# A memset of 256 spare words behind each gather on GpSimd, in the keys-and-values stage and in the gate stage of a graph network

## What is computed

```python
# layer 1, attention: per edge
k_e = k[src] + angle_emb @ We ; v_e = v[src] + angle_emb @ We
alpha = einsum('ehd,ehd->eh', q[dst], k_e) / sqrt(D)       # 8 heads of 16
# ... softmax over the edges of each target, then the sum of attn * v_e by target
# layer 3, gates: per edge
gates = softmax(concat([x_src, x_dst, x_edge]) @ W_gate + b_gate)
out = gates[:, 0:1] * x_src + gates[:, 1:2] * x_dst + gates[:, 2:3] * x_edge
segment_sum(out, col, num_segments=N)
```

## Time and profile before

| | |
|---|---|
| median of three runs | 7083.06 us (7050.15 to 7134.01) |
| span of the profiled execution | 7080.9 us; no other time of that execution is given |
| keys-and-values stage, first to last gather | 2370.6 to 3800.4 us |
| gate stage, first to last gather | 5607.2 to 7013.9 us |
| busy shares of the span | TensorE 59%, VectorE 42%, GpSimd 41%, ScalarE 18% |

### The profile page before, as it was taken

The page is one execution under the profiler, slowest core; times in us unless marked ns, Lnnn a source line. Parts: engine busy times, 40 slices in busy tenths (PEclk is TensorE's granted clock), DMA queues, the critical chain, the costliest instruction groups (busy, mean ns, idle before and its releaser), DMA issues.

```text
span 7080.9 us, 98147 instructions
## 1 busy us (share of the span) xinstructions
PE 4162.5 (59%) x25513; PEld 3308.9 (47%) x25514; DVE 2977.6 (42%) x8318; ACT 1295.5 (18%) x3253; POOL 2894.8 (41%) x2784
## 2 busy tenths in 40 slices
PE   1112000599898455555563664798899666666664
PEld 1001000366565455555553563465565666556654
DVE  3438201411313344444446677212312555555556
ACT  0001000000100211111111664200200322322222
POOL 6778777000000265555553565000000255555555
PEclk6555555799899777777776996899999755655555
DMA  9713000366463455555552451464364222222222
GB/s 361 267 61 135 6 0 0 103 198 192 141 195 118 111 160 158 154 150 156 155 162 89 125 148 30 137 197 138 131 196 145 64 78 78 78 78 79 79 78 69
DMA packets 447985, 885.48 MB, mean 125 GB/s; under 512 B 91722, under 2 KB 278572, under 8 KB 441502
## 3 DMA queue, kind: packets, MB, share of 16 engines
q1 hardware_dynamic: 333406, 608.36, 27.1%
q0 software_dynamic: 106912, 224.30, 11.9%
q10 hardware_dynamic: 7584, 51.91, 2.0%
HBM read 728.93 MB, written 155.35 MB: 125 GB/s over the span
## 4 chain that ended last, share of the span: by engine, by line
PE 33%; DVE 20%; issue 19%; another core or an unknown queue 15%; DVEq 6%; DMA 2%; ACT 2%; ACTq 1%; SPq 0%; POOL 0%; POOLq 0%
PE ps L836 23%; DVE work L1603 3%; PE ps L992 2%; DVE work L624 2%; PE ps L415 1%; DVE work L368 1%; DMA hw<-d_keys 1%; DVE work L1202 1%; DVEq L342 1%; PE ps L1184 1%; DVE hw L438 1%; PE ps L843 1%; PE ps L1182 1%; DMA work<-attr_dram 1%
## 5 line engine op out<-in xcount | busy, mean ns | idle before, releaser
L361 POOL DMA_INDIRECT work<-tab_kv,src_col x832 | 814.1, 978 | 1758.7 <-DMA tab_kv<-hw 1142.1
L361 POOL DMA_INDIRECT work<-tab_gate,src_col x832 | 795.5, 956 | 1795.5 <-DMA tab_gate<-logits 1183.3
L484 POOL DMA_INDIRECT d_adj<-logits,address x782 | 848.1, 1085 | 276.6 <-issue 238.8
L836 PE MATMUL ps<-hw 128*128 128x384 bf16 x5096 | 863.4, 330 | 50.4 <-DVE hw L815 37.1
L836 PE MATMUL ps<-hw,work 128*128 128x384 bf16 x5096 | 845.1, 326 | 0.0
L415 PE MATMUL ps<-work 128*128 128x136 f32 (+1 forms) x3328 | 655.0, 360 | 131.6 <-DVE acc L438 86.4
L836 PEld LDWEIGHTS ps<-hw 128*128 128x128 bf16 x5096 | 502.1, 99 | 383.1 <-issue 53.7
L415 PEld LDWEIGHTS ps<-work 128*128 128x128 f32 x3328 | 599.8, 265 | 165.4 <-issue 165.4
L875 DVE TENSOR_TENSOR work<-work,ps 128x128 f32 (+1 forms) x208 | 59.9, 288 | 1410.0 <-ACT work L867 1409.2
L836 PEld LDWEIGHTS ps<-hw,work 128*128 128x128 bf16 x5096 | 498.8, 98 | 317.7
L1168 PE MATMUL ps<-ident,work 128*128 128x128 f32 x832 | 177.1, 350 | 656.8 <-ACT work L1158 285.2
(11 more groups left out here) (389 smaller groups left out, 6581.4 us busy)
## 6 DMA issues: line engine op xcount, KB each, us to landing
hw<-d_adj SPq DMA_DIRECT2D x104, 800.0 KB, 4.3
work<-d_adj SPq DMA_DIRECT2D x104, 800.0 KB, 4.4
d_adj<-acc SPq DMA_DIRECT2D x52, 1568.0 KB
hw<-d_adj SPq DMA_DIRECT2D x104, 768.0 KB, 4.2
work<-d_adj SPq DMA_DIRECT2D x104, 768.0 KB, 4.3
work<-attr_dram SPq DMA_DIRECT2D x832, 64.0 KB
d_value<-work SPq DMA_DIRECT2D x208, 256.0 KB
work<-d_value SPq DMA_DIRECT2D x208, 256.0 KB, 2.7
```

Of the source, the lines that this page charges most:

```text
L361: pool.indirect_dma_start(rows[:, r * U + u, 0:width], None, table, bass.IndirectOffsetOnAxis(sources[:, at:at + 1], 0)).then_inc(rows_in[ ...
L484: pool.indirect_dma_start(d_adj, bass.IndirectOffsetOnAxis(address[:, tile:tile + 1], 0), counts[:, tile:tile + 1], None).then_inc(adj_out ...
L836: last = nc.tensor.matmul(at, adj_half[2 * s + hf][:, k, :], xs[:, b, :], start=b == 0, stop=b == BLOCKS - 1)
```

## The change

Behind each gather of both stages GpSimd now writes zeros into 256 words of each partition of address. The memset first waits for the memset before it (semaphore paced, wait value 0 left out).

```diff
+        pause = address[:, 0:2 * P]
...
                     pool.indirect_dma_start(rows[:, r * U + u, 0:width], None, table,
                                             bass.IndirectOffsetOnAxis(sources[:, at:at + 1], 0)).then_inc(rows_in[r], 16)
+                    wait(pool, sem("paced"), k * STEPS + at)
+                    pool.memset(pause, 0).then_inc(sem("paced"), 1)
```

To make room for that semaphore, one that nobody waited for is dropped (scores_ready, one increment on VectorE), beta_in and beta_ready become one (beta_dve, waited for at 1 and 2), and x_and_h, relu_ready and x_biased become one (x_added, waited for at GROUPS, 2 and 3 times GROUPS):

```diff
             dve.wait_ge(sem("kv_done"), ALL_PARTS)
-            dve.sem_inc(sem("scores_ready"), 1)
...
-            act.wait_ge(sem("beta_in"), 1)
+            act.wait_ge(sem("beta_dve"), 1)
...
-            dve.sem_inc(sem("beta_ready"), 1)
+            dve.sem_inc(sem("beta_dve"), 1)
...
-            act.wait_ge(sem("beta_ready"), 1)
+            act.wait_ge(sem("beta_dve"), 2)
...
-            dve.wait_ge(sem("x_and_h"), GROUPS)
+            dve.wait_ge(sem("x_added"), GROUPS)
...
-            dve.wait_ge(sem("relu_ready"), GROUPS)
+            dve.wait_ge(sem("x_added"), 2 * GROUPS)
...
-            dve.wait_ge(sem("x_biased"), GROUPS)
+            dve.wait_ge(sem("x_added"), 3 * GROUPS)
```

More of the change, by code:

```diff
@@ L1462, in att_end_dve @@
             p_skip.dve(dve, attention, behind=lambda g: dve.sem_inc(sem("mix_in"), 1))
-            nc.vector.tensor_tensor(stat[:, 0, :], stat[:, 0, :], stat[:, 6, :], ALU.add).then_inc(sem("beta_in"), 1)
+            nc.vector.tensor_tensor(stat[:, 0, :], stat[:, 0, :], stat[:, 6, :], ALU.add).then_inc(sem("beta_dve"), 1)
             dve.wait_ge(sem("beta_exp"), 1)
@@ L2030, in kv_ready @@
                 dve.sem_inc(sem("kv_ready"), 1)
-                nc.vector.tensor_tensor(group(x, g), group(x, g), group(h, g), ALU.add).then_inc(sem("x_and_h"), 1)
+                nc.vector.tensor_tensor(group(x, g), group(x, g), group(h, g), ALU.add).then_inc(sem("x_added"), 1)
             p_qkv.dve(dve, behind=kv_ready)
-            dve.wait_ge(sem("x_and_h"), GROUPS)
+            dve.wait_ge(sem("x_added"), GROUPS)
             att_dve(dve)
@@ L2054, in relu @@
             def relu(g):
-                nc.vector.tensor_scalar(group(t, g), group(t, g), 0.0, None, ALU.max).then_inc(sem("relu_ready"), 1)
+                nc.vector.tensor_scalar(group(t, g), group(t, g), 0.0, None, ALU.max).then_inc(sem("x_added"), 1)
             p_sage1.dve(dve, behind=relu)
-            dve.wait_ge(sem("relu_ready"), GROUPS)
+            dve.wait_ge(sem("x_added"), 2 * GROUPS)
             dve.sem_inc(sem("self2_ready"), GROUPS)
@@ L2060, in _ @@
             p_self2.dve(dve, behind=lambda g: nc.vector.tensor_tensor(
-                group(x, g), group(x, g), bias("L2_bn2", GROUP), ALU.add).then_inc(sem("x_biased"), 1))
-            dve.wait_ge(sem("x_biased"), GROUPS)
+                group(x, g), group(x, g), bias("L2_bn2", GROUP), ALU.add).then_inc(sem("x_added"), 1))
+            dve.wait_ge(sem("x_added"), 3 * GROUPS)
             dve.sem_inc(sem("dense_open"), 1)
```

## The result

The changed kernel takes **6841.38 us** (median of 6 runs, 6794.67 to 6870.51) against 7092.47 us for the kernel before in the same runs (6 runs, 7050.15 to 7134.01). The ratio is 0.9631, 95% interval 0.9577 to 0.9685: 3.7% faster. The forecast was 6840 us, from a mechanism that the experiments confirm in part; they also show that the gain exists only in one condition of the device.

What follows compares the result with a forecast made beforehand. Both gather stages were taken to be bound by waits, GpSimd pacing them while its gathers delay TensorE's signals. Savings of 134 + 110 = 244 us from 7080.9 gave 6837, forecast as 6840 us; range 6650 to 7380 us.

Steps and rivals of the forecast that it cites:

- Step 1: GpSimd's memset of 256 words behind each gather: about 0.31 us, at 0.83 ns a word.
- Step 2: Time between gather starts on GpSimd: 0.95 + 0.31 + 0.30 = 1.56 us; below 1.26, above 1.86.
- Step 3: TensorE's signals during gathers: at 1.56 us a backlog no longer grows, and signals pass as early in a burst.
- the early signals pass, so the queue is slightly overfull: Gather bursts at 1.25 us: TensorE's signals pass until a backlog has grown, as in a slightly overfull queue.
- only a dry queue frees the signals: Rival behind each burst: signals pass only when no gather has started for some 2.8 us; 450 us slower, 7533 us; chance 0.24.
- "remote" nearly gone from the waits and the chain's share below 8%: Sign of being right: waits for "remote" nearly vanish, and the chain's 15% for another core or unknown queue falls below 8%.
- Step 4: Both gather stages: GpSimd, never waiting, is the bound at 831 x 1.56 = 1296 us each, saving 244 us together.
- Step 5: Each memset's wait on GpSimd for the memset one pitch earlier, long over: 0 us.
- Step 6: VectorE beside the memset: its one-hot, 681 to 683 ns, is not slowed; 0 us.
- the upper bound of 258 us: VectorE held up for each memset's length while busy: 1664 x 0.31 x about 0.5 = 258 us.
- Step 7: Merged semaphores: as many waits at the same instants, one increment fewer on VectorE; 0 us.
- TensorE late by itself: Rival in the gather stages: TensorE's products really end when the waiters start; no change, 7083 us; chance 0.06.

Runs made afterwards that it cites:

- e4: Against the changed kernel: four fills of 256 words behind each part of four gathers instead of one behind each gather; 6999.8 us, ratio 0.9887 to the kernel before.
- e12: Against the changed kernel: fill of 8 words instead of 256; 7143.3 us, ratio 1.0012 to the kernel before.
- e2: Against the changed kernel: fill of 128 words instead of 256; 7081.2 us, ratio 1.0009 to the kernel before.
- e13: Against the changed kernel: two fills behind each part of four gathers instead of one behind each gather; 7032.6 us, ratio 0.9916 to the kernel before.
- e3: Against the changed kernel: two fills of 256 words behind each gather instead of one; 7313.5 us, ratio 1.0328 to the kernel before.
- e1: Against the changed kernel: fills removed, only the merged semaphores kept; 7084.7 us, ratio 1.0013 to the kernel before.
- e10: Against the changed kernel: no fill, each gather fetches half its row; 5885.1 us, ratio 0.9965 where the kernel before takes about 5900 us.
- e14: Against the changed kernel: no fill, half rows, run again where the kernel before takes about 7070 us; 7049.6 us, ratio 0.9959.
- e8: Against the changed kernel: no fill, GpSimd waits ahead of each part until the previous part's rows landed; 6908.5 us, ratio 1.1687 to the kernel before.

## Why the prediction was right, point by point

**Step 1, the fill.** Forecast 0.31 us, measured 0.330 us directly behind a gather (0.312 in e4, where three of four stand behind another fill). Near enough.

**Step 2, the pitch.** This term was mis-sized: 1.56 us forecast, 1.44 measured. I left the gap of 0.30 us whole ahead of the next gather; behind a fill it is 0.16. By the prediction's own rule for such a pitch (1.45 us, 1205 us a stage, 6656 us) the stage would take 831 x 1.44 = 1197 us.

**Step 3, what the pitch does to TensorE's signals.** Right for GpSimd, whose waits go, in the late condition; not right for the signals. A row of pitches shows the limit:

| pitch without waits, gathers of 0.95 us | GpSimd's waits for VectorE, us (both stages) | ratio |
|---|---|---|
| 1.23 (e12) | 365.5 + 375.7 | 1.0012 |
| 1.25 (before) | 390.2 + 389.9 | 1 |
| 1.33 (e2) | 340.1 + 270.0 | 1.0009 |
| about 1.4 (e13) | 251.0 + 186.2 | 0.9916 |
| 1.44 (the change) | 66.8 + 33.6 | 0.9631 |
| 1.57 on average (e4) | 39.7 | 0.9887 |
| 1.81 (e3) | 34.8 | 1.0328 |

Up to 1.33 us all of the rest goes into holes that were there anyway. Between 1.33 and 1.44 us most of the waits fall away. Beyond it only 100 us of waits are left to win, and a further fill costs more: e3's stages are 246 and 300 us longer than the change's. My reading "the early signals pass, so the queue is slightly overfull" fits such a limit, though no row shows a queue. What I gave 0.24, that only a dry queue frees the signals, is refuted by the change. From its keys-and-values stage:

```profile
2984.08 0.95 POOL L362 DMA_INDIRECT work<-tab_kv,src_col  x1 [0.16 <-issue]
2984.86 0.69 DVE L1202 TENSOR_TENSOR work<-ps,work 128x512 f32<-128x512 f32 x1 [4.16 <-remote]
...
2985.52 0.95 POOL L362 DMA_INDIRECT work<-tab_kv,src_col  x1 [0.16 <-issue]
2986.97 0.95 POOL L362 DMA_INDIRECT work<-tab_kv,src_col  x1 [0.16 <-issue]
2987.06 0.60 ACT L1160 ACTIVATE work<-ps 128x512 f32<-128x512 f32 x1 [6.23 <-remote]
```

The gathers follow each other at 1.44 us, and both signals arrive among them, with no pause of 2.8 us. But they arrive late. I had expected "remote" nearly gone from the waits and the chain's share below 8%; ScalarE's waits fell only from 763.8 to 743.0 us, and the chain's share is 14%. That the time came out so near in spite of it is partly luck: it was enough that each delay got shorter. The remote waits of the gather stages are gone only with more rest (e3, e4).

**Step 4, the sum.** Forecast 1296 us in both stages; measured 1299.0 and 1246.5. The first agreement is luck, made of two errors. GpSimd's own terms in keys and values are 829.2 of gathers (mean 0.997 us each, longer than the 0.95 taken), 832 x 0.330 = 275 of fills, 132 of gaps and 67 of waits for VectorE, together 1303 us. In the gate stage 809.1 + 275 + 133 + 34 = 1251 us. So the pitch is 0.12 us shorter than forecast (100 us a stage), and longer gathers and remaining waits give 100 us of it back in the first stage and 50 in the second. The total, 291 us against 244, came out 47 us better. The medians differ by 251 us, nearer to the forecast, because the profiled execution of the change was the fastest of its six. One support of step 4 was misread: of the two uses of L1580 that are 4.02 us apart, the first did wait, 1.74 us for remote and until 2.93 us behind a burst. The forecast did not rest on it, as 4.3 us of TensorE are below 6.24 as well.

**Step 5, the new wait.** GpSimd sat idle 0.8 us ahead of all 1664 fills. Right.

**Step 6, VectorE beside the fill.** Its one-hot took 687 ns in the mean of all 520, in the kernel before and in the changed one. Right: 0 us; the upper bound of 258 us was far off.

**Step 7, the merged semaphores.** 0 forecast; e1 gives 1.0013 (0.998 to 1.0046). Right.

**The rival "TensorE late by itself"** got 0.06, and was held to be excluded by the stage without gathers. It has part of the truth. Nothing in this program's instructions differs between 7070 us and 5904 us, so the lateness needs a cause outside of it; yet within the late condition GpSimd's indirect transfers and their rest decide how large it is. The Trainium skill, Perfetto Trace Analysis, Tensor Engine Instruction, says that the recorded end of a matmul is an estimate and that its semaphore goes out only when PSUM has acknowledged the bytes. An error of the estimate alone is not the explanation here: the same products with the same shapes are followed by their user after 0.03 us in one condition and 4.5 us in the other. Whether the product itself, its acknowledgement or its signal is what comes late, no trace here can tell; "late signals" stands for all three.

**Open.** What the condition is (other work on the device, or a setting of it) no run here shows. Whether a rest without writes does the same in the late condition was met by no run: in every run of that condition the length of a fill and the words it writes go together. Nor was a mean pitch between 1.44 and 1.57 us tried, which might be faster than the change. A rest among the 782 scatters, where the late condition costs some 530 us, was not tried.

## What to carry to other kernels

When the chain of waits names "another core or an unknown queue" in a program of one core, look who is the real partner in the code, and where the lateness ends: here it ended with GpSimd's indirect transfers, and, in the late condition, slowing GpSimd down by 0.2 us per gather made the program 3.7% faster. Look for the limit with several sizes, since half the pause gave nothing and double the pause cost 3.3%. Lay waits side by side only over stretches of the same work, and look at their number as well as their sum: here ScalarE's sum hardly moved (763.8 to 743.0 us) while each wait got shorter (9.2 to 6.4 us). And measure the kernel before again each time: a remedy for a condition of the device is a loss (3.9% here) when the condition is absent.

## What the runs showed of the hardware that was not expected

- The same program took 7068 and 5904 us in groups of runs minutes apart; most of the difference lies in the stages with indirect transfers from GpSimd, and shows as waits for "remote" after TensorE.
- A fill on GpSimd takes 120 ns for 8 words, 218 for 128, 330 for 256, directly behind a gather. The gap ahead of a gather is 0.30 us behind another gather and 0.16 us behind a fill, so the first 0.14 us of a fill are free.
- Halving each gathered row took the DMA share from 0.53 to 0.40 and left the gather at 0.95 us on GpSimd and changed the time by 0.35% and 0.41% (e10, e14).
- Waiting on GpSimd for a part's rows to land holds it for 3.25 us a part in keys and values and 2.53 us in the gate stage (e8); the whole costs 17% of this kernel's time in the prompt condition.
